# A Mamba block and a mixture-of-experts FFN on one core: GpSimd's products of B and u in pairs, and the tiles dealt anew

## The reference, cut to what matters

```python
# layer 1, Mamba, d_inner 512, d_state 16
xn = rmsnorm(layernorm(x)); xs, res = split(xn @ W_in)
xs = silu(causal_conv4(xs)); dt, B, C = split(xs @ W_x); dt = softplus(dt @ W_dt)
h[t] = exp(A * dt[t]) * h[t-1] + dt[t] * B[t] * xs[t]      # for each of 512 d and 16 n
y[t] = sum over n of h[t] * C[t];  out = (y * silu(res)) @ W_out
# layer 2: expert e has tokens 512e to 512e+511, d_ff 704
out = (silu(x @ w1[e]) * (x @ w3[e])) @ w2[e]
```

## Time and profile before

| | us |
|---|---|
| median of 3 runs | 978.57 (977.22 to 978.98) |
| the profiled execution's own time | 979.27 |
| its span, first to last instruction | 977.5 |
| busy: PE, DVE, POOL, ACT | 912.5, 900.1, 893.5, 745.8 |
| granted TensorE clock, mean | 0.982 |

### The profile page before, as it was taken

One profiled execution on the slowest core, in us unless ns is written; L12 is line 12 of the kernel. 1 busy time (PEld: TensorE's weight loads), 2 busy tenths in 40 slices (PEclk: granted clock), 3 DMA queues, 4 the chain that ended last, 5 costly groups with the idle time before them and its releaser, 6 DMA issues. The chain is left out here.

```text
span 977.5 us, 13189 instructions
## 1 busy us (share of the span) xinstructions
PE 912.5 (93%) x4204; PEld 601.2 (62%) x4204; DVE 900.1 (92%) x1000; ACT 745.8 (76%) x1356; POOL 893.5 (91%) x425
## 2 busy tenths in 40 slices
PE   6989988999999999999999999999999998677988
PEld 4555455655766566755766567655667557554777
DVE  5889899899999999999999999999999989988983
ACT  4577877888779878888879787888788876567771
POOL 1498899999999999999999999999999999998970
PEclk9998999999999999999999999999999999699999
DMA  5580145011651039111471037310580117401100
GB/s 176 227 295 22 43 164 226 1 68 59 259 202 46 23 114 353 54 68 46 182 293 40 29 102 274 144 68 0 188 331 1 47 60 264 153 22 59 52 1 22
DMA packets 43477, 116.82 MB, mean 120 GB/s; under 512 B 8592, under 2 KB 27024, under 8 KB 34192
## 3 DMA queue, kind: packets, MB, share of 16 engines
q1 hardware_dynamic: 41552, 115.94, 31.9%
q10 hardware_dynamic: 1856, 0.04, 0.1%
HBM read 110.21 MB, written 5.77 MB: 119 GB/s over the span
## 5 line engine op out<-in xcount | busy, mean ns | idle before, releaser
L701 DVE TENSOR_TENSOR_SCAN ring<-ebank,state,ring 128x512 f32<-128x512 f32 (+1 forms) x544 | 626.4, 1203 | 36.8 <-ACT ebank L864 28.7
L553 POOL TENSOR_TENSOR hc<-ring,c_all 128x1024 f32<-128x1024 f32 (+1 forms) x256 | 600.4, 2367 | 18.4 <-DVE ring L701 10.7
L864 ACT ACTIVATE ebank<-dt_,a_neg 128x512 f32<-128x512 f32 (+1 forms) x544 | 353.0, 662 | 143.0 <-DVE ring L701 139.5
L1323 PEld LDWEIGHTS ybank<-ident,hc 128*128 128x128 f32 x1920 | 221.0, 142 | 95.4 <-issue 58.0
L542 POOL TENSOR_TENSOR ring<-b_all,u 128x1024 f32<-128x1024 f32 x110 | 261.1, 2374 | 9.9 <-DVE taken L644 9.5
L1323 PE MATMUL ybank<-ident,hc 128*128 128x128 f32 x1920 | 245.2, 276 | 23.0 <-POOL hc L553 14.3
L681 DVE TENSOR_TENSOR ring<-b_all,ubank 128x1024 f32<-128x1024 f32 x144 | 172.0, 1195 | 0.0
L1248 PE MATMUL gbank<-xT,w 128*128 128x512 f32 x280 | 132.0, 603 | 7.1 <-DVE hb L811 6.8
L1248 PE MATMUL gbank<-xT,w_a 128*128 128x512 f32 x256 | 120.1, 606 | 8.0 <-DVE dt_ L669 4.4
L1248 PE MATMUL gbank<-xs,w_a 128*128 128x512 f32 x224 | 100.8, 593 | 0.7 <-ACT sres L896 0.7
L1248 PEld LDWEIGHTS gbank<-xT,w 128*128 128x128 f32 x280 | 50.2, 192 | 64.0 <-issue 46.0
(11 more groups left out here) (164 smaller groups left out, 854.9 us busy)
## 6 DMA issues: line engine op xcount, KB each, us to landing
b_all<-bc_kept SPq DMA_DIRECT2D x32, 1024.0 KB, 6.7
c_all<-bc_kept SPq DMA_DIRECT2D x32, 1024.0 KB, 8.4
w<-in_L_ffn_w_dram SPq DMA_DIRECT2D x16, 640.0 KB, 4.9
w_a<-in_L_attn_W_in_dram SPq DMA_DIRECT2D x7, 1024.0 KB, 4.8
w_a<-wc_kept SPq DMA_DIRECT2D x7, 1024.0 KB, 4.9
w2s<-in_L_ffn_w_dram SPq DMA_DIRECT2D x8, 640.0 KB, 9.3
xin<-in_L_attn_x_dram SPq DMA_DIRECT2D x9, 512.0 KB, 3.8
x<-in_L_attn_x_dram SPq DMA_DIRECT2D x7, 512.0 KB, 6.4
```

The source lines that it names most:

```text
L553: ch_ok.by(e.tensor_tensor(tile_of(hc, c, q)[:, 0:many, :], tile_of(ring, c, q)[:, 0:many, :], c_all[:, n:n + many, tok], ALU.mult))
L701: h_ok.by(e.tensor_tensor_scan(row, e_of(c, j), row, initial=all_states[:, first:first + 1], op0=ALU.mult, op1=ALU.add))
L864: e_ok.by(e.activation(e_of(c, j), dt_[:, d, tok], ACT.Exp, scale=a_neg[:, d, n0 + n:n0 + n + 1]))
L1323: last = e.matmul(ybank[:, cols(b)], hc[:, q % HC, n, cols(b)], ident[:, :], is_transpose=True, start=(k == 0 and n == 0 and b == 0), stop ...
```

## The change

In chunks 1 to 6 (`steady`) POOL makes the products of tiles 10 and 11, 14 and 15, and 22 and 23 as one instruction of 128x2048 each (`bu_two`), and u of two d blocks in one instruction of 128x1024 (`u_two`): blocks 2 and 3 behind tile 2, blocks 0 and 1 of the next chunk behind tile 28. `POOL_BU` still has 14 tiles: 4, 17, 18, 21 and 27 go to DVE, and 2, 15, 19, 20 and 26 come to POOL. DVE makes the product of tile 21 not right behind the scans of tile 20 but behind `hidden_tail`. On ACT `residual(0, 1)` at q = 5 becomes `residual(0)` at q = 4 and `residual(1)` at q = 5. The table of chunk 0 takes over `u_two(0)`, that of chunk 7 `u_two(2)`.

```diff
-    POOL_BU = (1, 4, 7, 10, 11, 14, 17, 18, 21, 22, 23, 24, 27, 29)
+    POOL_BU = (1, 2, 7, 10, 11, 14, 15, 19, 20, 22, 23, 24, 26, 29)
+    TWO = (10, 14, 22)
+    BEHIND = 21
...
+        def steady(c):
+            return 0 < c < E - 1
...
@@ gpsimd
+            def u_two(d):
+                def job(c, i):
+                    for k in (d, d + 1):
+                        wait_dt(e, c, k)
+                    xs_ok.wait(e, c)
+                    ub_ok.wait(e, c - 1, d + 2)
+                    e.tensor_tensor(u[:, d:d + 2, :], dt_[:, d:d + 2, :], xs[:, d:d + 2, :], ALU.mult).then_inc(u_ok.sem, 2)
+                return job
...
+            def bu_two(c, q):
+                d, n, many, tok = spot(c, q)
+                u_ok.wait(e, c, d + 1)
...
+                cb, qb = tile_before(c, q + 1, RING)
+                ch_ok.wait(e, cb, qb + 1)
+                st_ok.wait(e, cb, qb // 2 + 1)
+                dst = ring[:, q % RING:q % RING + 2, :, :].rearrange("p a n t -> p (a n) t")
+                e.tensor_tensor(dst, b_all[:, n:n + 2 * NG, :], u[:, d, :].unsqueeze(1).broadcast_to([P, 2 * NG, TC]), ALU.mult
+                                ).then_inc(bup_ok.sem, 2)
...
                 r = q + AHEAD
-                if r < Q and r in pool_bu(c):
+                if steady(c) and r in TWO:
+                    bu_two(c, r)
+                elif r < Q and r in pool_bu(c) and not (steady(c) and r - 1 in TWO):
                     bu(c, r)
...
-            table = [(4, "scan", u_of(ND - 1)), (10, "back", back), (21, "next", front), (24, "front", u_of(0)),
-                     (27, "front", u_of(1)), (29, "front", u_of(2))]
-            table0 = [(3, "late", u_of(1)), (7, "late", u_of(2)), (10, "late", u_of(3)), (23, "next", front),
-                      (27, "front", u_of(0)), (28, "front", u_of(1)), (29, "front", u_of(2))]
-            run(table, table0, [(4, "scan", u_of(ND - 1))], [], group)
+            table = [(2, "scan", u_two(2)), (10, "back", back), (21, "next", front), (28, "front", u_two(0))]
+            table0 = [(3, "late", u_of(1)), (7, "late", u_of(2)), (10, "late", u_of(3)), (23, "next", front), (28, "front", u_two(0))]
+            run(table, table0, [(2, "scan", u_two(2))], [], group)
...
@@ vector
+            def bu_behind(c, i):
+                if steady(c):
+                    bu(c, BEHIND)
...
-                elif q + 1 < Q and q + 1 in dve_bu(c) and (c, q) != (E - 1, QH + 1):
+                elif q + 1 < Q and q + 1 in dve_bu(c) and (c, q) != (E - 1, QH + 1) and not (steady(c) and q + 1 == BEHIND):
                     bu(c, q + 1)
...
-                     (20, "back", hidden_tail), (21, "back", hidden(2)), (22, "back", hidden(3)), (23, "back", hidden(4)),
+                     (20, "back", hidden_tail), (20, "scan", bu_behind), (21, "back", hidden(2)), (22, "back", hidden(3)), (23, "back", hidden(4)),
...
@@ scalar
-                     (3, "front", before_conv(3)), (3, "front", convolved(0)), (4, "front", convolved(1)), (5, "front", convolved(2)), (5, "back", residual(0, 1)),
+                     (3, "front", before_conv(3)), (3, "front", convolved(0)), (4, "front", convolved(1)), (4, "back", residual(0)), (5, "front", convolved(2)), (5, "back", residual(1)),
```

More of the change, by code:

```diff
@@ L543, in bu @@
                                           u[:, d, tok].unsqueeze(1).broadcast_to([P, many, tok.stop - tok.start]), ALU.mult))
+            def bu_two(c, q):
+                d, n, many, tok = spot(c, q)
+                u_ok.wait(e, c, d + 1)
+                if d == 0:
+                    b_in[n // SG].wait(e, c)
+                    b_in[(n + NG) // SG].wait(e, c)
+                cb, qb = tile_before(c, q + 1, RING)
[4 more added lines that the diff above has]
+                                ).then_inc(bup_ok.sem, 2)
             def group(c, q):
```

## The result

The changed kernel takes 1000.59 us in the median (998.78 to 1000.99), the one before 978.43 beside it (977.22 to 978.98): ratio 1.0225, 95% interval 1.0207 to 1.0242. It is slower, as forecast, but by 22.2 us and not by 9.5, and outside the range of 982 to 992.5.

What follows compares the result with a forecast made beforehand. It took a loop through POOL, PE, ACT and DVE, nearly without slack, as the bound. Chunk 1's 1.8, five loops of 1.6 (8.0) and -0.3 at the end gave +9.5 us: median 988.1 us, range 982 to 992.5.

Steps and rivals of the forecast that it cites:

- its five parts: Loop from tile 21's scans through POOL, PE, ACT and DVE: 2.54 + 79.49 + 2.43 + 17.65 + 10.43 = 112.54 us.
- 79.49 + 1.76 = 81.25: POOL, `hc` of 21 to `hc` of 12: one more product, 2.32 us, less four groupings at 0.14 each.
- its own engine has just made the one: `bu_two` on POOL: its wait for `hc` was given no cost, POOL having just made that `hc`.
- 112.53 + 1.76, less the 0.2 us: Whole loop: the period becomes 114.1 us, or +1.6 us a chunk.
- The 0.2 us of GATE 3: PE at GATE 2 and 3: 3.80 us against DT 0's 3.60, read as waiting for a bank ACT reads late.
- Tile 2's product: Now from POOL behind `hc` of 31: ready at 499.2, some 0.1 us behind the end of tile 1's scans.
- That is worth nothing to the loop: ACT's `residual(0)` a tile earlier: DVE's 0.70 us idle at tile 6 goes, with no gain, POOL being still behind DVE.
- Chunk 1: POOL's stretch from `hc` of 9 to `hc` of 12 grows by 1.5 to 2.0 us, taken as 1.8.
- The end: Chunk 7, POOL full and its lists unchanged: two `u_two` give 0.3 us back.
- The fast rival: POOL is the limit and PE has cover at tile 12: 4.5 to 7 us saved, 971.5 to 974; chance 0.10.
- ACT and PE caught nothing up: Rival that they catch up between tiles 12 and 21: half of 9.5 us, about 983 (979 to 984.5); chance 0.10.
- The worse rival: Scans 9 to 11 pass POOL through a late product, or a pair saves nothing: 992 to 996 us; chance 0.10.

Runs made afterwards that it cites:

- experiments 1: Changed kernel with the pair of tiles 14 and 15 taken apart, tile 15's product made behind `hc` of 12: 977.63 us, ratio 0.9991 to the kernel before.
- 2: Changed kernel with PE's DT 0 moved one tile earlier, ahead of the sum of tile 12: 978.34 us, ratio 0.9997 to the kernel before.
- experiment 4: Kernel before with tile 14's product made twice on POOL in chunks 1 to 6: 1000.47 us, ratio 1.0230 to the kernel before.
- experiment 3: Changed kernel with 22 unread transposes on PE ahead of the sum of tile 12 in chunks 1 to 6: 991.70 us, ratio 1.0136 to the kernel before.
- experiment 8: Kernel before with products 10, 14 and 22 also waiting for the `hc` just ahead on POOL: 978.96 us, ratio 1.0008 to the kernel before.

## Why the prediction was right in its sign and wrong in its size

- The loop of the kernel before, its five parts and the place of the loss are as read; experiments 1, 2 and 4 each show it from another side.
- "79.49 + 1.76 = 81.25": measured 81.92, so this term was 0.67 us a chunk too small. The price of the pair (4.50, measured 4.51) and of `u_two` held. The term left out is the start of a pair behind its own `hc`. I named that wait ("its own engine has just made the one") and put it at nothing; it is 0.28 and 0.33 us, 0.6 a chunk, more than the 0.14 that a pair saves.
- "112.53 + 1.76, less the 0.2 us": this is the step that failed. I took PE's 17.65 us from the sum of 12 to TAIL as fixed but for GATE 3, whatever stood ahead of them. They took 18.82, since the clock was at its lower level for 3.4 us at their start. I forecast the idle that comes before it and did not ask what it does to the clock. It costs 1.38 us a chunk (experiment 3), 8 of the 12 us that I missed; the pairs are most of the other four. The trace of before had it to see. Its page shows lower levels at both ends of the span, where PE has gaps, and at the start of chunk 7 a like sum of eight transposes takes the same 1.97 us behind an idle:

```profile
PE   6989988999999999999999999999999998677988
...
PEclk9998999999999999999999999999999999699999
```

```profile
835.71 1.97 PE L1323 MATMUL ybank<-ident,hc 128*128 128x128 f32 x8 [3.52 <-POOL hc L553]
```

- The 0.2 us of GATE 3 came back as said, 3.80 to 3.60.
- POOL's idle before tile 21 is 3.05 us for my 2.7, with another 0.8 at tile 19; PE's before the sum of 12 is 2.73 for 1.6.
- Tile 2's product came in time (DVE waits for decays there, not for it), POOL met no scan up to tile 11, and DVE's 0.70 us at tile 6 went.
- "That is worth nothing to the loop", of the split residual: wrong. It is worth 0.19 us a chunk and 2.0 us in all, through the very bank of GATE 3 that I had noted as read late.
- Chunk 1: 2.9 us for 1.8; in experiment 3, where the clock stays up, it is 1.8. The end: +0.3 for -0.3.
- The fast rival has nothing for it, and ACT and PE caught nothing up between tiles 12 and 21 (10.43 us from TAIL on, as before). The worse rival, 992 to 996, was the nearest and still 4.6 us short. No scan passed POOL up to tile 11, so its main cause was not there; its other, that a pair saves nothing, came true, for 0.6 us a chunk.

## What to carry to other kernels

When a change makes an engine wait on a loop that has no slack, reckon what the wait does to that engine, not only how long it is: TensorE may come back from an idle at its lower clock, and cheap work put into the gap, or better a matmul group moved there, can be worth more than its own length suggests (here 8.9 us for 2.6 in each of six chunks). A grouped instruction stands whole at the place of its first member: count what it now stands ahead of, and which waits of its second member it takes over. And two edits that gain nothing or little alone can gain together when each uncovers the other's wait.

## What the runs showed that I had not expected

- TensorE's clock went to its lower level for 3.4 us at an idle of 2.6 to 2.8 us in 11 of 12 chunks (chunks 1 to 6 of the changed kernel and of experiment 4), and did not in one with the same 2.60 us. In the seven kernels here with `u_two` it did so too at an idle of 2.7 us late in chunk 0.
- 2.6 us of useless transposes in each of six chunks saved 8.9 us.
- A POOL instruction of 128x2048 that waits for the instruction ahead of it on POOL starts 0.28 to 0.33 us later than in a full queue, one of 128x1024 0.2 us (experiment 8).
